# Buffers of their own for the last four row tiles of a cross-attention and quantized-FFN block, another order of its first loads, and newly written orders of all engines

## The reference, cut to what matters

```
def block(x, ctx, mask, ...):
    q = layernorm(x) @ wq + bq ; k = ctx @ wk + bk ; v = ctx @ wv + bv     # 16 heads of 32
    p = softmax(where(mask == 0, 1e-9, q k^T / sqrt(32)))
    x = x + (p v) @ wo + bo
    y = layernorm(x)
    h = gelu(actq(rms(y)) @ weightq(w1)^T + b1)                            # 512 -> 2048
    return x + actq(rms(h)) @ weightq(w2)^T + b2                           # 2048 -> 512
# actq: a row scaled to its own maximum, rounded to -128..127
# weightq: the whole matrix scaled by its mean |w|, rounded to -1, 0, 1
```

## Time and profile before

| what | us |
|---|---|
| runs | 657.62, 657.68, 659.87 (median 657.68) |
| the profiled execution, its own time | 658.44 |
| span of its instructions | 656.6 |
| mean granted TensorE clock | 0.997 |

### The profile page before, as it was taken

How to read it: one execution, slowest core, us unless ns; L and a number is a source line. 1 busy time by engine, 2 the same in 40 slices (tenths; PEclk the granted TensorE clock), 3 DMA queues, 4 the chain that set the end, 5 groups by cost and what they waited for, 6 DMA issues and landing times.

```text
span 656.6 us, 14114 instructions
## 1 busy us (share of the span) xinstructions
PE 633.1 (96%) x4904; PEld 424.6 (65%) x4904; DVE 576.7 (88%) x1062; ACT 530.0 (81%) x1450; POOL 517.0 (79%) x653
## 2 busy tenths in 40 slices
PE   8888999999999999999999999999999999899996
PEld 7656886665566776666667766666766766556532
DVE  6678889998999989999799989999898889999995
ACT  2379678887898878888988878888888889988782
POOL 3198985979866999669966989669967878889966
PEclk9999999999999999999999999999999999999999
DMA  8982420423124433072244533053333212524236
GB/s 286 404 277 119 127 42 9 105 43 102 33 58 121 120 73 73 10 182 82 41 73 100 143 72 73 9 153 80 72 73 73 69 28 73 115 58 117 57 61 176
DMA packets 109285, 65.38 MB, mean 100 GB/s; under 512 B 90855, under 2 KB 90855, under 8 KB 108575
## 3 DMA queue, kind: packets, MB, share of 16 engines
q1 hardware_dynamic: 108159, 64.49, 37.7%
q10 hardware_dynamic: 1056, 0.00, 0.1%
HBM read 35.12 MB, written 8.39 MB: 66 GB/s over the span
## 4 chain that ended last, share of the span: by engine, by line
PE 54%; POOL 18%; DVE 13%; issue 5%; DMA 4%; ACT 4%; SPq 2%; POOLq 0%; DVEq 0%
PE ps_a L561 19%; PE ps_y L698 10%; PE ps_z L675 9%; PE ps_t L634 6%; POOL prob L2246 4%; PE ps_s L624 3%; POOL hid L2257 3%; PE ps_a L646 3%; DVE hs L1620 2%; POOL q_h L2262 2%; DMA raw_wk_h<-in_L_ffn_w_dram 2%; DVE hid L1612 2%; ACT prob L1133 2%; POOL xn L2202 2%; PE ps_a L595 2%
## 5 line engine op out<-in xcount | busy, mean ns | idle before, releaser
L1133 ACT ACTIVATE prob<-ps_s,nmax 128x120 f32<-128x120 f32 x512 | 178.8, 375 | 31.4 <-DVE nmax L1566 25.0
L2246 POOL TENSOR_TENSOR prob<-prob,pinv 128x480 f32<-128x480 f32 x128 | 128.8, 1012 | 51.1 <-DVE pinv L1571 50.5
L675 PE MATMUL ps_z<-w1T,q_xT 128*128 128x512 fp8e4 x476 | 122.7, 380 | 4.4 <-DVE hid L1612 3.5
L1133 ACT ACTIVATION_READ_ACCUMULATOR prob<-ps_s,nmax 128x1 f32 x512 | 112.7, 220 | 0.0
L698 PE MATMUL ps_y<-w2T,q_hT 128*128 128x512 fp8e4 x448 | 104.0, 379 | 0.3 <-DMA q_hT<-q_h 0.3
L1612 DVE SCALAR_TENSOR_TENSOR hid<-ps_z,y_deq,b_row 128x512 f32<-128x512 f32 x119 | 88.0, 740 | 12.9 <-PE ps_z L675 10.8
L1109 ACT COPY probT<-ps_t 120x512 f32<-120x512 f32 x128 | 76.7, 599 | 26.8 <-PE ps_t L634 23.4
L1563 DVE COPY_PREDICATED_SCALAR ps_s<-hidden_key,masked_c 128x480 f32 x128 | 90.5, 707 | 3.4 <-PE ps_s L624 3.4
L1566 DVE TENSOR_REDUCE nmax<-ps_s 128x4 f32<-128x480 f32 x128 | 84.1, 657 | 4.4
L634 PE MATMUL ps_t<-ident,prob 128*120 128x128 f32 x512 | 78.2, 275 | 2.4 <-POOL prob L2246 2.3
L634 PEld LDWEIGHTS ps_t<-ident,prob 128*120 128x120 f32 x512 | 59.8, 137 | 24.0 <-issue 6.2
(11 more groups left out here) (207 smaller groups left out, 1379.7 us busy)
## 6 DMA issues: line engine op xcount, KB each, us to landing
x<-in_x_dram SPq DMA_DIRECT2D x32, 256.0 KB, 3.0
out_dram<-x SPq DMA_DIRECT2D x32, 256.0 KB, 2.7
xn<-in_x_dram SPq DMA_DIRECT2D x7, 1024.0 KB, 6.5
hid<-in_L_ffn_w_dram SPq DMA_DIRECT2D x4, 1024.0 KB, 8.7
ctx_k<-in_ctx_dram SPq DMA_DIRECT2D x8, 240.0 KB, 3.9
ctx_k<-in_mask_Bx1xSxS_ik_dram SPq DMA_DIRECT2D x7, 240.0 KB, 3.5
xn<-in_x_dram SPq DMA_DIRECT2D x4, 256.0 KB, 4.8
x<-in_L_xattn_wq_dram SPq DMA_DIRECT2D x1, 1024.0 KB, 8.4
```

What stands on the lines that cost most here:

```text
L675: last = nc.tensor.matmul(bank[:], q_xT[:, k % 3, i], w1T[:, i, c * CH:(c + 1) * CH], start=(i == 0), stop=(i == KD - 1))
L1133: last = nc.scalar.activation(prob[:, n % 3, g * S2:(g + 1) * S2], ps_s[n % HG][:, g * S2:(g + 1) * S2], ACT.Exp, bias=nmax[:, n % 4, g:g ...
L2246: gp.tensor_tensor(pr, pr, pinv[:, n % 4].unsqueeze(2).to_broadcast([P, HG, S2]), ALU.mult).then_inc(s["prob_ready"], 1)
```

## The change

1. Tiles 28 and 29 get FFN buffers over `wv_h` and `wv_l`; tile 28's codes go over `wk_l`; the transposed codes of tiles 28 and 29 go over the upper half of `wk_h` and `wk_l`. The waits named above fall away; in their place `evac_up(28, 0)` and `evac_up(29, 0)` wait until the last query projection is done, as those of tiles 30 and 31 did.
2. The first loads go out in another order: wk before wq, the pieces 1, 3, 0, 2, and mask 0 and bo behind the pieces. ACT waits for the third tile of x before it issues bq and bk.
3. All five lists of calls are written anew. No call is added or taken away: PE has 534 calls before and after, ACT 458, DVE 687, POOL 350, SP 160. The order of use of the PSUM banks stays.

The code outside of the lists:

```diff
+        q_h_28 = over("q_h_28", "wk_l", [P, F], BF16)
+        q_hT_own = [over("q_hT_28", "wk_h", [P, KF, P], BF16, 2 * F), over("q_hT_29", "wk_l", [P, KF, P], BF16, 2 * F)]
-        hid_last = [... over("hid_30", "wq_h", ...), over("hid_31", "wq_l", ...)]
+        hid_last = [... over("hid_28", "wv_h", ...), over("hid_29", "wv_l", ...), over("hid_30", "wq_h", ...), over("hid_31", "wq_l", ...)]
         def rounded(k):
-            return q_h_tail if k == NT - 3 else q_h[:]
+            return (q_h[:], q_h_28[:], q_h_tail)[max(k - NT + 5, 0)]
         def hidden(k):
-            return hid_last[k - LAST] if k >= LAST else hid[:, k % 2]
+            return hid_last[k - NT + 4] if k >= NT - 4 else hid[:, k % 2]
         def turned_h(k):
-            return q_hT_last[k - LAST] if k >= LAST else q_hT[:, k % 2]
+            if k >= LAST:
+                return q_hT_last[k - LAST]
+            return q_hT_own[k - NT + 4][:] if k >= NT - 4 else q_hT[:, k % 2]
...
             def turn_h(k):
-                if k < LAST:
+                if k < NT - 4:
                     wait(sp, "y_full", k - 1)
...
             def round_h(k):
                 act.wait_ge(s["h_magic"], k + 1)
-                if k == NT - 4:
-                    act.wait_ge(s[f"qhT{(k - 1) % 2}_in"], 16 * ((k - 1) // 2 + 1))
...
+            act.wait_ge(s["first2_in"], 16)
             for v, dst in ((bq, bq_col), (bk, bk_col)):
...
             def evac_up(k, c):
-                    if k >= LAST:
+                    if k >= NT - 4:
                         dve.wait_ge(s["a_full"], AJ_N[("q", NB - 1, G - 1)] + 1)
...
             def round_h(k):
-                if k == LAST:
-                    wait(pool, "qh_act", 1)
-                else:
+                if k != LAST:
                     pool.wait_ge(s["sq_done"], k + 1)
```

More of the change, by code:

```diff
@@ L829, in _ @@
             turn_xn(2, 2)
-            ffn_up(1, 1)
             attend(3)
@@ L870, in _ @@
             project_out(5)
+            ffn_up(4, 0)
             turn_probs(27)
+            project_q(2, 3)
             ffn_down(2, 0)
-            ffn_up(4, 0)
-            project_q(2, 3)
             ffn_up(4, 1)
@@ L1226, in _ @@
             evac_piece(0, 2)
-            exps(1)
             evac_turn(("c", 1, 0))
-            evac_probs(0)
             evac_piece(1, 0)
             sum_abs(4)
+            evac_piece(1, 2)
+            exps(1)
+            evac_probs(0)
             exps(2)
-            evac_piece(1, 2)
+            evac_keys(1)
+            evac_piece(2, 0)
             exps(3)
-            evac_piece(2, 0)
-            evac_probs(1)
             sum_abs(6)
@@ L1268, in _ @@
             evac_piece(5, 2)
+            exps(10)
             evac_piece(6, 0)
@@ L1490, in _ @@
             exps(126)
+            evac_probs(124)
             evac_o(30)
-            evac_probs(124)
             exps(127)
+            gelu(27)
             evac_probs(125)
-            gelu(27)
             evac_probs(126)
@@ L1989, in _ @@
-                h_scale(4 * a - 1)
-                evac_up(4 * a, 1)
+                softmax_max(16 * a + 14)
+                invert_sums(16 * a + 12)
                 softmax_max(16 * a + 15)
                 invert_sums(16 * a + 13)
+                h_scale(4 * a - 1)
                 ln2_scales(4 * a + 1)
-            evac_down(18)
+                evac_up(4 * a, 1)
             evac_up(20, 2)
             invert_sums(94)
+            invert_sums(95)
+            evac_down(18)
             oT_low(22)
-            invert_sums(95)
@@ L2011, in _ @@
             invert_sums(98)
-            ln2_scales(22)
-            evac_up(21, 0)
             h_scale(20)
-            evac_up(21, 1)
-            invert_sums(99)
             evac_down(19)
-            evac_up(21, 2)
+            oT_low(23)
+            softmax_max(100)
             xT_low(7, 2)
-            oT_low(23)
             evac_up(21, 3)
-            softmax_max(100)
             softmax_max(101)
             residual(23)
-            h_scale(21)
+            softmax_max(102)
             evac_up(22, 0)
@@ L2027, in _ @@
             xT_low(7, 3)
+            invert_sums(99)
+            h_scale(21)
+            add_bv(7)
             invert_sums(100)
-            invert_sums(101)
-            add_bv(7)
-            softmax_max(102)
+            ln2_stats(23)
             softmax_max(103)
             evac_up(22, 1)
-            ln2_stats(23)
             oT_low(24)
+            invert_sums(101)
+            ln2_scales(23)
             evac_down(20)
-            ln2_scales(23)
             invert_sums(102)
+            invert_sums(103)
@@ L2128, in _ @@
             h_scale(26)
+            oT_low(29)
             invert_sums(123)
@@ L2442, in _ @@
             normalize(95)
+            h_factor(19)
             y_factor(21)
             normalize(96)
+            add_bo(23)
+            y_factor(22)
             normalize(97)
-            y_factor(22)
-            h_factor(19)
+            add_b2(21)
+            normalize(98)
             round_x(22)
-            normalize(98)
+            add_b2(22)
+            round_h(20)
+            h_factor(20)
             normalize(99)
-            round_h(20)
-            add_bo(23)
-            h_factor(20)
+            add_bo(24)
@@ L2468, in _ @@
             normalize(106)
-            add_b2(23)
-            round_x(24)
             round_h(22)
             normalize(107)
-            h_factor(22)
-            normalize(108)
-            normalize(109)
             y_factor(24)
             add_b2(24)
-            add_bo(26)
+            normalize(108)
+            h_factor(22)
+            normalize(109)
             normalize(110)
+            normalize(111)
+            round_x(25)
+            round_h(23)
+            normalize(112)
@@ L2524, in _ @@
             add_bo(31)
+            round_h(28)
             y_factor(30)
-            round_h(28)
+            h_factor(27)
             round_x(31)
-            h_factor(27)
             y_factor(31)
```

829 lines of the change are left out of this document (417 added, 412 removed).

## The result

The changed kernel takes 655.34 us (median of 6; 653.62 to 656.01) beside 658.81 us for the kernel before (median of 6): ratio 0.9946, interval 0.9928 to 0.9964, so 3.6 us less (2.4 to 4.7). The forecast was a sum of -4.2 us and 653.5 us. Its 653.5 stood on a median of 657.68 us before; beside the change, the kernel before took 1.1 us more than that, so it is the two differences that can be compared. The granted clock matters for what follows: five executions of the changed kernel had a mean of 0.995 to 0.997 and took 655.22 to 656.01 us, the sixth had 1.000 and took 653.62.

What follows compares the result with a forecast made beforehand. Loads and POOL were taken to bound the start, PE the middle, DVE nearly the end. Start -1.6, middle -1.3, loop 0 and late -1.3 sum to -4.2 us, from a 657.68 us median to 653.5, range 647 to 657.

Steps and rivals of the forecast that it cites:

- Buffers: Last tiles: the six waits that fall away were not the last to end, so their removal gains 0.
- Start: First 60 us, where PE waits for loads and POOL: 2.06 us earlier, 0.5 given back, -1.6 us.
- (a): Start: mask 0 and bo behind w1's last piece, which comes 1.24 us earlier; holding back bq and bk costs 0.
- (b): Start: POOL's `normalize(0)` no longer idles for its inverse, now ahead of `softmax_max(1)`; 0.82 us gained.
- (c): Start: DVE's `split_wo` seemed to hold up POOL's `normalize(0)` by 2.09 us; that cost stays, now at `round_piece(2)`.
- (d): Start: ACT's `sum_abs(7)` is late next, between the last piece's two `evac_piece`; a quarter given back, 0.5 us.
- Middle: Tile 1's way down, at 156 us: most of PE's 1.57 us wait in `turn_ctx(3)` for `evac_down(1)` goes, -1.3 us.
- Loop: Repeated turns: -0.8 from `q_xT` waits at `ffn_up(4a-3, 0)`, +0.8 from `evac_up(4a, 1)` coming later; sum 0.
- the slower rival: Loop: `evac_up(4a, 1)` has no slack, so DVE's lateness stands on PE four times; 662.7 us, chance 0.20.
- Late: `ffn_up(26, 0)`: its 1.33 us wait for `evac_up(25, 3)` goes, with `project_out(27)` now between; -1.3 us.
- The clock: Start: a halved clock falling on `project_ctx(0, "v")` doubles its 3.60 us of products; +3.6, 657.1 us, chance 0.08.
- Nothing gained: Whole kernel: PE and DVE keep the same work, the start's gain is waited away under DVE; 657.7 us, chance 0.20.

Runs made afterwards that it cites:

- later_busy: scale_later with 22 transposes added on PE ahead of `total_weights(0)`; 654.34 us, ratio 0.9953.
- two_fills: later_busy with 18 more transposes on PE ahead of `turn_piece(3, (0, 1))`; 654.39 us, ratio 0.9946.
- no_start: The changed kernel with the first 98 us as before; 655.51 us, ratio 0.9963.
- buffers_alone: The kernel before with only the changed kernel's buffers of the last four tiles and its waits; 658.01 us, ratio 0.9994.
- middle_alone: The kernel before with the new orders from about 98 to 181 us alone (tiles 1 to 5); 657.23 us, ratio 0.9984.
- middle_loop: The kernel before with the new orders from about 98 to 483 us, tiles 1 to 5 and the loop's four turns; 657.53 us, ratio 0.9983.
- late_alone: The kernel before with the new orders from about 483 us to the end and the new buffers; 657.51 us, ratio 0.9990.
- scale_later: The changed kernel with DVE's scale of bq moved behind `xT_low(0, 3)` and the split of wq; 656.78 us, ratio 0.9961.
- bias_first: The changed kernel without ACT's wait for the third x tile ahead of the bias loads; 654.59 us, ratio 0.9939.

## Why the prediction came out right, and where its terms were off

**Buffers, 0.** Right: -0.4 us (-0.9 to +0.2), and the wait of the earlier trace rows is unchanged.

**Start, -1.6.** Measured -0.9 (-1.4 to -0.3): right in sign, put too high. The step that failed is (a): "holding back bq and bk ... so 0", under the cover of transposes. The last piece of w1 does land more than the expected 1.2 us earlier: in later_busy ACT's sum over it begins at 24.67 us and names no DMA. But holding back the biases put 3.1 us on DVE, then on PE, whose clock fell behind it, and ACT's sum stands behind the evacuations that PE feeds. The cover did not hold: the bytes were counted, not what stands behind the biases on DVE. (b) is right, 0.82 us of idle gone. (c) is right: the price of the split moved to the next rounding, 4.10 for 1.98 us. The Trainium skill, page SBUF — State Buffer, section Who interferes with whom, has it that a VectorE instruction with two inputs in SBUF contends with a GpSimd instruction that reads SBUF, over a pair of ports that is locked exclusively; the trace agrees, 1.98 + 2.28 = 4.26 against 4.10. (d) was put too low: `total_weights(1)` comes at 59.82 instead of 58.62 us, because `sum_abs(7)`, between the two halves of the last piece, starts at 56.22 instead of 54.50. With the 0.2 us that were ahead at `total_weights(0)` it gave back 1.4 us by there, not 0.5. The clock is not the reason: between these two points two_fills, without a fall, takes 30.59 us, the old start without one (no_start, buffers_alone) 29.25 and 29.27.

**Middle, -1.3.** By middle_alone's time, -1.05 (-1.6 to -0.5), it fits; by the traces of the whole change it was put too low: PE's waits there fell by 3.2 - 1.1 = 2.1 us. The mechanism, `turn_ctx(3)` and `evac_down(1)`, gave 1.2 of it; two kinds of wait with 0.6 us each, for POOL's probabilities and for DVE's values, were not looked at and went too. The bound of -1.57 was that of one wait, not of the stage. The two more table loads show in no wait of PE, as said.

**Loop, 0.** Right in sum, by luck in its parts: middle_alone -1.05, middle_loop -1.1. PE has no wait of `ffn_up(4a, 2)` for `evac_up(4a, 1)` in any turn, so the +0.8 did not come; the slower rival's place held, with 0.46 to 0.72 us of slack in the four turns, where the forecast saw none (`ln2_scales` took 1.51 us there, not 1.88). The -0.8 did not come either: the waits for a landing `q_xT` left `ffn_up(4a-3, 0)`, and two came at `ffn_up(4a-1, 0)`, 0.51 and 0.54 us at 241.51 and 390.96.

**Late, -1.3.** Mis-sized: the wait went, and the next came 10 us on, 1.3 us in `attend`. The step that failed is what is late next: the forecast looked at DVE, 18.72 of 20 us busy in that window, and it was ACT, which its own had at 19.05. By PE's waits -0.4 us is left, by late_alone's time -0.7.

**The last 45 us.** Right: the changed kernel is 3.21 us ahead at `residual(30)` and 2.97 us ahead at PE's last products.

**The clock.** Its rival had the right mechanism and a wrong place. A fall did come beyond 35 us, 0.63 and 0.51 from 54 to 58 us in the changed kernel, not on `project_ctx(0, "v")` but on the turning of the last piece; two_fills shows that it is all but hidden there. Of a context projection at the lower clock only scale_later has one, and it lost 1.7 us. The rival had PE waiting ahead of `total_weights(0)`; it waited in the first projection of q, and the other fall came there, from 20 to 24 us. And that POOL's rounding hides a fall on `project_q(0, 3)` holds in part only: about 0.7 us of it came through in the old start. The changed kernel's one execution at a clock of 1.000 was 1.6 us faster than any other of it, so its falls may cost as much; one execution doesn't settle that.

**Nothing gained.** This rival took PE's busy time for its measure. That time stayed within 0.4 us and the kernel gained 3.6, out of PE's idle time.

So that the sum came out within 0.6 us is in part luck: a start and an end that were put too high stand against a middle that was put too low. What stays open is which of (a) to (d) makes up the start's 0.9 us: no profile of the new start without those added transposes has a clock of 1.000.

## What to carry to other kernels

Before an early load is held back, look at what stands behind its consumer in that engine's queue: 4 KB of biases cost DVE 3.1 us, and the same new load order under the old engine orders cost 8.8 us. When a wait is priced, sum all waits of its stage, and ask of every engine which is late next; here the fullest of all was passed over. A fallen clock is a loss only as far as the others wait for PE. Before two profiles are compared, compare their granted clocks: the same instructions ran 2.75 us apart. Filling PE's idle time with empty transposes holds the clock, but look at the whole stage again, since the next wait can bring the fall back.

## What the hardware showed that was not expected

Small loads behind large ones. Landing times from issue, us, for the bias loads (2 KB each), and the packets of ACT's DMA queue; in the kernel before, then in the changed kernel:

```profile
q10 hardware_dynamic: 1056, 0.00, 2.9%
...
bq_col<-in_L_xattn_bq_dram ACTq DMA_DIRECT2D x1, 2.0 KB, 3.9
bk_col<-in_L_xattn_bk_dram ACTq DMA_DIRECT2D x1, 2.0 KB, 4.9
```

```profile
q1 hardware_dynamic: 3187, 6.23, 90.8%
q10 hardware_dynamic: 1056, 0.00, 3.4%
...
bq_col<-in_L_xattn_bq_dram ACTq DMA_DIRECT2D x1, 2.0 KB, 8.3
bk_col<-in_L_xattn_bk_dram ACTq DMA_DIRECT2D x1, 2.0 KB, 10.7
```

The 1056 packets of 4 bytes landed in 4.9 us when they were issued ahead of most loads, and in 10.7 us behind them. That is 66 packets on each of 16 engines; an estimate from these rows: if each took turns with one packet of the loads (6.23 MB / 3187 = 1955 bytes, 0.08 us at an engine's share of 400 GB/s), 66 x 0.08 = 5.3 us would be added, and 5.8 were. The Trainium skill, page DMA: Bandwidth & Descriptors, section Queues, rings and completion order, says that a DMA engine goes round between its queues packet by packet. Its packets hold several descriptors each; whether those that the profile counts are the same, no run here shows.

TensorE's granted clock was 0.50 (1.2 instead of 2.4 GHz) from 48 to 50 us in scale_later, behind PE's wait in `turn_piece(2)`, and 1.00 in bias_first behind the same wait. Even one and the same kernel doesn't fall alike each time: executions of the kernel before had a mean granted clock of 0.994 to 1.000. The old start, with the same instructions, ended up to 2.75 us apart in the profiles (74.67 and 77.42 us at `residual(0)`), the earliest without a fall, the latest with the longest.
